# Transformer block on one core: x turned by VectorE and on-chip transfers instead of TensorE, all engine orders laid anew

## The chip, the cores and the metric

The kernel runs on one core of a Trainium2 chip. A core has five engines that run their own instruction streams and wait for each other by semaphores: TensorE (PE; its weight loads are shown as PEld), VectorE (DVE), ScalarE (ACT), GpSimd (POOL) and SyncE (SP), which here only issues transfers. The metric is the device time of one launch in microseconds (us), the median of several runs.

## The reference

For each of 32 batches of 256 tokens with 128 features, in float32:

```python
x = x + layernorm(attention(layernorm(x), Wqkv, Wo))
x = x + layernorm(tanh(layernorm(x) @ weight @ aux_weight1 @ aux_weight2 + bias))
```

Attention has 8 heads of 64. Wqkv (1536x128) gives q, k and v; a table of sines and cosines is added to q and k; scores = q k^T / 8 with a causal mask, softmax, times v; Wo (128x512) brings the 512 head values back to 128. The layernorms have no weights, epsilon is 1e-5.

## The kernel before, in words

A batch's 256 tokens are two tiles of 128 rows, so most tiles are 128 partitions by 2 x 128 columns. The 8 heads are worked in two units k = 0, 1 of two pairs j = 0, 1 of two heads each.

What happens to a batch b, with the function of each step:

- SP loads x twice, into `x_in` (for the norm) and later `x_res` (for the residual). DVE takes mean and variance (`stats_x`, `take_moments`), POOL makes 1/sqrt(var + eps) and writes the normalised `xn` (`norm_x`).
- PE turns `xn` with two 128x128 transposes into `misc_bank` (`turn_x`, by `turn_rows`, L941). ACT copies the result rounded to `xt_hi` (`keep_x_hi`, L307) and DVE writes the remainder `xt_lo` (`keep_x_lo`, L681). The two parts let q, k and v be computed in the fast format with three products each (`make_qk`, L896 to L898; `make_vals`, L867 to L869).
- `make_qk(b, k, j)` fills the one `qk_bank`; DVE adds the sine table and frees it (`keep_qk`, L643). `make_scores` (L881) writes two score banks; DVE masks and takes the row maximum (`row_max`, L633), ACT takes the exponentials and row sums (`exps`, L265), DVE inverts the sums.
- The probabilities are scaled by the inverse sums: of pair 0 by DVE (`scale_probs`, L659), of pair 1 by POOL (L423).
- PE turns each pair's probabilities in 12 transposes of 64-row blocks (`turn_probs`, L921), ACT copies them out (`keep_turned`, L283 and L285), PE multiplies with v (`make_heads`, L935). The heads of unit 0 are copied out by DVE (`keep_heads`, L669), those of unit 1 by ACT (L295). The turned probabilities and the heads share two PSUM banks, so each `turn_probs` of pair 0 waits for the copy of the heads before it.
- `make_attn` (L996) multiplies with Wo into `misc_bank`; ACT copies it (`keep_attn`, L331), DVE takes statistics and normalises (`norm_attn`), POOL adds the residual (`make_x1`, L482).
- The second half: DVE statistics, POOL normalises (`norm_y`), PE turns y (`turn_y`), ACT copies (`keep_y`), PE multiplies with the three weights fused into one (`make_ffn`), ACT takes tanh, DVE statistics, POOL normalises and adds (`norm_ffn`, `make_out`), SP stores.

Every engine has its order written out by hand: a `begin`, a `slot(b, k)` for each batch and unit, in which neighbouring steps belong to different batches (b+2 for the norm of x, b-3 for the last norm), and an `end`. `all_slots` runs the first four batches straight, the middle ones in a loop of two batches, and the last one by `end`. An engine executes its list in order: whatever waits holds up all that stands behind it. `misc_bank` is shared by x turned, v, y turned, the feed-forward product and the attention product.

Of the kernel before, what the change touches and what calls it, by code (L numbers as in the profile page):

```python
# [7 lines left out]
ALU = mybir.AluOpType  # L8
# [6 lines left out]
P = 128  # L15
# [7 lines left out]
class Batch:  # L23
# [39 lines left out]
def build_block(nc, x, w_qkv_t, w_o_t, w1_t, w2, w3, bias, out, H):  # L63
# [17 lines left out]
    with ExitStack() as ctx:  # L81
# [32 lines left out]
        half_power, eps = sb("half_power", [P, TT]), sb("eps", [P, TT])  # L114
# [7 lines left out]
        xt_hi, xt_lo = two("xt_hi", [P, T], F32R), two("xt_lo", [P, T], F32R)  # L122
        vals = two("vals", [P, TT, F])
# [27 lines left out]
        x_turned, x_hi_kept, x_lo_kept = sem("x_turned"), sem("x_hi_kept"), sem("x_lo_kept")  # L151
        attn_made, attn_kept, x1_made, out_made = sem("attn_made"), sem("attn_kept"), sem("x1_made"), sem("out_made")
# [41 lines left out]
        def _(sp):  # L194
# [7 lines left out]

            def slot(b, k):
                if k == 0 and b.plus(3).exists():

                    wait(sp, norms["x"]["normed"], b.times(1, 2))
                    load(b.plus(3), x_in, x_loaded)
                if k == 0 and b.plus(1).exists():

                    wait(sp, x1_made, b.times(1))  # L210
                    load(b.plus(1), x_res, res_loaded)
                if k == 1 and b.plus(-2).exists():
                    c = b.plus(-2)
                    sp.wait_ge(out_made, c.times(1, 1))
                    sp.dma_start(rows(out_dram, c), x2[c.parity][:, :, :]).then_inc(stored[c.parity], 16)

            load(first, x_in, x_loaded)
            sp.dma_start(ident[:, :], ident_dram).then_inc(ident_in, 16)
            sp.dma_start(pe[:, :], pe_dram).then_inc(pe_in, 16)
            sp.dma_start(mask[:, :], mask_dram).then_inc(mask_in, 16)  # L220
# [8 lines left out]
            sp.dma_start(wo[:, :, :], w_o_t.rearrange("(c f) e -> f c e", f=P)).then_inc(wo_in, 16)  # L229
            for b in range(-1, 4):  # L230
                for k in range(2):
                    slot(Batch(b // 2, b % 2, B), k)
# [4 lines left out]
            for b in range(B - 4, B + 2):  # L237
                for k in range(2):
                    slot(Batch(b // 2, b % 2, B), k)
# [5 lines left out]
        def _(act):  # L245
            for i in range(3):
                part = slice(i * F, (i + 1) * F)
                act.dma_start(w_raw[:, part], w_qkv_t[:, part]).then_inc(w_in[i], 16)
# [19 lines left out]

            def keep_vals(b, t):
# [18 lines left out]
            def keep_heads(b):  # L288

                if not b.exists():  # L290
                    return
                act.wait_ge(heads_made, units(b, 2))

                wait(act, attn_made, b.times(1, -1))
                nc.scalar.copy(heads_t[b.parity][:, 2:4, :], heads_bank[:, :].rearrange("p (j t) -> p j t", j=2)  # L295
                               ).then_inc(heads_kept[1], 1)

            def keep_x_hi(b):
                if not b.exists():
                    return  # L300
                act.wait_ge(x_turned, b.times(1, 1))

                wait(act, y_turned, b.times(1, -2))
# [3 lines left out]
                nc.scalar.copy(xt_hi[b.parity][:, :], misc_bank[:, 0:T]).then_inc(x_hi_kept, 1)  # L307
# [803 lines left out]
```

## Time and profile before

| | |
|---|---|
| median of 3 runs | 556.6 us (556.47 to 557.93) |
| profiled execution, device time | 557.18 us |
| its span, first to last instruction | 555.3 us |
| PE busy | 523.5 us, 94% of the span |
| DVE busy | 468.8 us, 84% |
| ACT busy | 410.9 us, 74% |
| POOL busy | 398.9 us, 72% |
| mean granted TensorE clock | 0.982 of full |

The profile is of one execution. Around the span lie 1.9 us in which no engine runs an instruction (557.18 - 555.3). Busy is the time in which at least one instruction of the engine runs; a busy PE includes the filling and emptying of its pipeline, so PE's busy share stays high even in short stalls, and the starts of its groups of matmuls tell more than its busy time.

### The profile page before, as it was taken

The page shows a single profiled execution, that of the slowest core. Times are in us where ns is not written, and L with a number is a line of the kernel's source. Part 1 is how long each engine was busy: PE and PEld are TensorE (multiplying, and loading weights), DVE is VectorE, ACT ScalarE, POOL GpSimd, SP SyncE. Part 2 cuts the span into 40 slices and gives each one's busy share as a digit, 9 for nine tenths or more (in the row PEclk, how much of TensorE's full clock was granted, in tenths as well). Part 3 has the DMA queues.
Part 4 walks back from the last instruction along what each step waited for, and adds up shares of the span by engine and source line. Part 5 has one row for each costly group of instructions (what it writes and reads, how often), then busy time and mean ns, then how long its engine had stood idle before and what let it go on. Part 6 is the DMA issues. An engine that isn't in the chain of part 4 may idle for free.

```text
span 555.3 us, 18471 instructions
## 1 busy us (share of the span) xinstructions
PE 523.5 (94%) x5363; PEld 427.2 (77%) x5363; DVE 468.8 (84%) x2063; ACT 410.9 (74%) x1507; POOL 398.9 (72%) x650
## 2 busy tenths in 40 slices
PE   8799999999999999999999999999999999999771
PEld 4588888788888878888887887888788888878650
DVE  4988898888889888888988888898888889888723
ACT  2777878778787877878787787877778787777730
POOL 3535777777777777777778777777877777785644
PEclk9999999999999999999999999999999999999966
DMA  5100011100001010000101010010000001100000
GB/s 161 30 2 21 11 31 30 30 19 28 20 18 28 28 28 19 28 26 12 28 28 28 19 28 21 17 28 28 28 19 28 26 12 28 28 19 12 21 11 19
DMA packets 27964, 14.57 MB, mean 26 GB/s; under 512 B 1699, under 2 KB 27430, under 8 KB 27942
## 3 DMA queue, kind: packets, MB, share of 16 engines
q1 hardware_dynamic: 27510, 13.51, 8.5%
q10 hardware_dynamic: 432, 0.79, 0.4%
q8 instruction: 11, 0.18, 0.1%
q14 instruction: 11, 0.09, 0.1%
HBM read 10.09 MB, written 4.19 MB: 26 GB/s over the span
## 4 chain that ended last, share of the span: by engine, by line
PE 82%; ACT 9%; issue 4%; DVE 3%; DMA 1%; POOL 1%; ACTq 0%; POOLq 0%; DVEq 0%
PE turned_and_heads L935 17%; PE scores L881 15%; PE misc_bank L996 11%; PE turned_and_heads L921 9%; PE qk_bank L896 6%; ACT probs L265 5%; PE qk_bank L898 4%; PE qk_bank L897 4%; PE misc_bank L867 4%; PE misc_bank L979 3%; PE misc_bank L869 3%; PE misc_bank L868 3%; ACT vals L275 2%; ACT pt L285 1%; PE misc_bank L977 1%
## 5 line engine op out<-in xcount | busy, mean ns | idle before, releaser
L265 ACT ACTIVATE probs<-scores,neg_max 128x256 f32<-128x256 f32 (+1 forms) x512 | 209.3, 428 | 32.0 <-DVE neg_max L633 31.9
L633 DVE CUSTOM_DVE_ANT_0 scores<-scores,mask 128x256 f32<-128x256 f32 (+1 forms) x512 | 166.2, 386 | 3.2 <-PE scores L881 0.9
L643 DVE TENSOR_TENSOR qk<-qk_bank,pe 128x512 f32<-128x512 f32 x128 | 87.4, 683 | 32.9 <-PE qk_bank L898 25.3
L881 PE MATMUL scores<-qk 64*128 64x256 f32 (+1 forms) x1024 | 107.2, 337 | 5.5 <-ACT probs L265 2.5
L423 POOL TENSOR_TENSOR probs<-probs,inv_sum 128x512 f32<-128x512 f32 x126 | 101.6, 827 | 12.8 <-DVE inv_sum L649 12.8
L265 ACT ACTIVATION_READ_ACCUMULATOR probs<-scores,neg_max 128x1 f32 x512 | 108.8, 213 | 0.0
L881 PEld LDWEIGHTS scores<-qk 64*128 64x128 f32 x1024 | 88.5, 188 | 16.0 <-issue 9.8
L935 PE MATMUL turned_and_heads<-pt,vals 128*64 128x256 f32 (+1 forms) x1024 | 99.3, 337 | 1.5 <-ACT pt L285 1.5
L935 PEld LDWEIGHTS turned_and_heads<-pt,vals 128*64 128x64 f32 x1024 | 64.8, 138 | 28.3 <-issue 2.8
L283 ACT COPY pt<-turned_and_heads 128x512 f32<-128x512 f32 x128 | 76.7, 599 | 11.1 <-PE turned_and_heads L921 11.0
L896 PE MATMUL qk_bank<-xt_hi,w_hi 128*128 128x256 f32 x256 | 81.2, 317 | 2.0 <-DVE qk L643 1.2
L921 PEld LDWEIGHTS turned_and_heads<-ident,probs 64*128 64x128 f32 x1536 | 58.5, 140 | 30.0 <-issue 22.1
L921 PE MATMUL turned_and_heads<-ident,probs 64*128 64x64 f32 x1536 | 75.9, 232 | 4.7 <-ACT pt L285 3.5
L659 DVE TENSOR_TENSOR probs<-probs,inv_sum 128x512 f32<-128x512 f32 (+1 forms) x128 | 77.2, 643 | 0.0
L633 DVE DVE_READ_ACCUMULATOR2_ANT neg_max<- 128x1 f32 x512 | 71.8, 140 | 0.0
L898 PE MATMUL qk_bank<-xt_hi,w_lo 128*128 128x256 f32 x256 | 71.4, 279 | 0.0
L897 PE MATMUL qk_bank<-xt_lo,w_hi 128*128 128x256 f32 x256 | 71.3, 279 | 0.0
L996 PE MATMUL misc_bank<-wo,heads_t 128*128 128x128 f32 x512 | 65.1, 280 | 0.6 <-ACT ffn_th L322 0.6
L996 PEld LDWEIGHTS misc_bank<-wo,heads_t 128*128 128x128 f32 x512 | 59.6, 191 | 5.6 <-issue 3.9
L896 PEld LDWEIGHTS qk_bank<-xt_hi,w_hi 128*128 128x128 f32 x256 | 48.0, 188 | 12.3 <-issue 7.7
L285 ACT COPY pt<-turned_and_heads 128x256 f32<-128x256 f32 x128 | 51.0, 398 | 0.0
L275 ACT COPY vals<-misc_bank 128x512 f32<-128x512 f32 x64 | 39.4, 616 | 15.2 <-PE misc_bank L869 15.2
(87 smaller groups left out, 863.2 us busy)
## 6 DMA issues: line engine op xcount, KB each, us to landing
x_in<-in_x SPq DMA_DIRECT2D x32, 128.0 KB, 2.2
x_res<-in_x SPq DMA_DIRECT2D x32, 128.0 KB, 2.1
out_x<-x SPq DMA_DIRECT2D x32, 128.0 KB, 1.8
w_raw<-in_w_qkv_t ACTq DMA_DIRECT2D x3, 256.0 KB, 3.7
pe<-pe_table SPq DMA_DIRECT2D x1, 256.0 KB, 5.6
wo<-in_w_o_t SPq DMA_DIRECT2D x1, 256.0 KB, 4.0
mask<-causal_mask SPq DMA_DIRECT2D x1, 128.0 KB, 5.5
w_sb<-in_w SPq DMA_DIRECT2D x2, 64.0 KB, 3.8
```

Source lines behind the costliest of these rows:

```text
L265: ins = nc.scalar.activation(probs[k][j][:, h, lo:hi], s_bank[j][:, h, lo:hi], ACT.Exp, bias=neg_max[k][j][:, i:i + 1], scale=-1.0, accum_ ...
L423: ins = nc.gpsimd.tensor_tensor(some, some, inv, ALU.mult)
L633: ins = nc.vector.tensor_tensor_reduce(some, some, mask[:, t * P:2 * P], -1.0, HIGHEST, ALU.add, ALU.min, neg_max[k][j][:, i:i + 1])
L643: nc.vector.tensor_tensor(qk[j][:, :], qk_bank[:, :], pe[:, :], ALU.add).then_inc(qk_kept, 1)
L659: ins = nc.vector.tensor_tensor(some, some, inv, ALU.mult)
L881: ins = mm(s_bank[j][:, h, at:at + k_hi], qk[j][r, q_lo:q_lo + P], qk[j][r, T:T + k_hi], start=(at == 0), stop=True, skip_group_check=True)
L896: mm(to, w_hi[:, f], hi[:, :], start=True, stop=False)
L897: mm(to, w_hi[:, f], lo[:, :], start=False, stop=False)
L898: ins = mm(to, w_lo[:, f], hi[:, :], start=False, stop=True)
L921: ins = nc.tensor.transpose(turned_banks[:, f, n * D:(n + 1) * D], some[r, h, lo:lo + P], ident[r, r])
L935: ins = mm(heads_bank[h * D:(h + 1) * D, to], vals[b.parity][:, s, f:f + D], rhs[j][:, h, :], start=(s == 0), stop=(s == 1))
L996: ins = mm(misc_bank[:, t * E:(t + 1) * E], heads_t[b.parity][:, p, t * P:(t + 1) * P], wo[:, p, :], start=(p == 0), stop=(p == PAIRS - 1))
```

## The change

What it does, part by part:

1. **x turned without PE.** For every batch but the first, DVE transposes `xn` in 32x32 blocks in place of each block (`turn_x_blocks`, one instruction of 128x256), and SP issues 16 transfers within SBUF, one for each block position (i, j), that move block (j, i) of `x_blocks` to (i, j) of `xt` (`move_x`). Each moves 32 partitions x 2 x 32 floats. `keep_x_hi` and `keep_x_lo` read `xt` in SBUF, not `misc_bank`. PE's `turn_x` remains for batch 0 alone, and steps that shared `misc_bank` with it lose that wait.
2. **Scaling of pair 0** goes from DVE (two instructions a unit) to ACT (four a unit, in place).
3. **The copy of unit 1's heads** goes from ACT to DVE.
4. **All orders** of `slot`, `begin` and `end` are written anew on all five engines. Loads and stores on SP are one batch later or share the slot with `move_x`.
5. **Start:** the exponential's table is loaded by a dummy instruction; the first two thirds of the weights are loaded by SP, identity, mask and Wo by ACT; the first `make_qk` waits for the parts of the weights one by one.
6. **End:** the last attention product is written to `qk_bank`, without waiting for `misc_bank`; 31 products of zeros (`warm_up`) are placed among PE's last steps, where there were none; at the start there are 17 for 15.

The core of the diff (the orders of `end` and of POOL are left out):

```diff
+            def move_x(b):
+                if not b.exists() or b.is_below(1):
+                    return
+                sp.wait_ge(x_blocked, b.times(1))
+                parts = [slice(n, n + 32) for n in range(0, P, 32)]
+                for i in parts:
+                    for j in parts:
+                        sp.dma_start(xt[b.parity][i, :, j], x_blocks[b.parity][j, :, i]).then_inc(x_moved[b.parity], 16)
...
             def slot(b, k):
+                if k == 0:
+                    load_x(b.plus(3))
+                    load_res(b)
+                else:
+                    move_x(b.plus(2))
+                    store(b.plus(-3))
...
+            def scale_probs(b, k):
...
+                act.wait_ge(inv_found, pairs(b, k, 1))
+                for t, (lo, hi) in enumerate(((0, T), (T, SC))):
+                    for h in range(2):
+                        some, i = probs[k][0][:, h, lo:hi], 2 * t + h
+                        ins = nc.scalar.mul(some, some, inv_sum[k][0][:, i:i + 1])
+                ins.then_inc(scaled[0], 1)
...
-                act.wait_ge(x_turned, b.times(1, 1))
-                wait(act, y_turned, b.times(1, -2))
+                    wait_moved(act, b)
...
+            def turn_x_blocks(b):
...
+                dve.wait_ge(norms["x"]["normed"], b.times(1, 1))
+                if not b.is_below(3):
+                    wait_moved(dve, b.plus(-2))
+                nc.vector.transpose(x_blocks[b.parity][:, :, :], xn[b.parity][:, :, :]).then_inc(x_blocked, 1)
```

The new order of a batch on ACT, in the names of the code (b is the slot's batch; slot k = 0, then k = 1): exps(b-1,1,0), keep_y(b-3), exps(b-1,1,1), keep_turned(b-1,0,0), tanh(b-3), scale_probs(b-1,1), keep_turned(b-1,0,1), keep_attn(b-2); exps(b,0,0), exps(b,0,1), keep_vals(b,0), keep_turned(b-1,1,0), keep_x_hi(b+1), scale_probs(b,0), keep_turned(b-1,1,1), keep_vals(b,1).
On POOL: norm_y(b-2), norm_x(b+2), scale_probs(b,0), norm_ffn(b-3); scale_probs(b,1), rstd_attn(b-1), make_out(b-3), make_x1(b-1).

PE in the middle of the kernel, before: from the transposes of x to the second score group of a unit. The names in brackets are the semaphores waited for.

```order
L941 MATMUL misc_bank<-ident,xn 128x128 [waits vals_kept,x_normed]
L941 MATMUL misc_bank<-ident,xn 128x128
L941 MATMUL misc_bank<-ident,yn 128x128 [waits vals_kept,y_normed]
L941 MATMUL misc_bank<-ident,yn 128x128
L921 MATMUL turned_and_heads<-ident,probs 128x64 [waits pt1_kept,scaled1,pt0_kept]
L921 MATMUL turned_and_heads<-ident,probs 128x64 x11
L881 MATMUL scores<-qk 128x256 [waits exps_done,qk_kept]
L881 MATMUL scores<-qk 128x256
L881 MATMUL scores<-qk 128x128 x2
L881 MATMUL scores<-qk 128x256 [waits exps_done,qk_kept]
```

And the same stretch of PE after:

```order
L977 MATMUL turned_and_heads<-ident,probs 128x64 [waits heads_kept0,pt1_kept,scaled0,pt0_kept]
L977 MATMUL turned_and_heads<-ident,probs 128x64 x11
L934 MATMUL scores<-qk 128x256 [waits exps_done,qk_kept]
L934 MATMUL scores<-qk 128x256
L934 MATMUL scores<-qk 128x128 x2
L934 MATMUL scores<-qk 128x256 [waits exps_done,qk_kept]
L934 MATMUL scores<-qk 128x256
L934 MATMUL scores<-qk 128x128 x2
L977 MATMUL turned_and_heads<-ident,probs 128x64 [waits pt1_kept,scaled1,pt0_kept]
L977 MATMUL turned_and_heads<-ident,probs 128x64 x11
L920 MATMUL misc_bank<-w_hi,xt_hi 128x512 [waits vals_kept]
```

The transposes of x are gone, and the scores of unit 1 now stand between the two groups of turned probabilities, ahead of the second half of v.

DVE in the middle, before: the last rows of a batch's unit 1.

```order
L633 ISA neg_max 128x1
L569 BN_STATS attn_stats<-attn 128x6 x2
L649 RECIPROCAL inv_sum<-row_sum 128x4
L582 BN_AGGR attn_moments<-attn_stats 128x2 x2
L659 TENSOR_TENSOR probs<-probs,inv_sum 128x2x256
L659 TENSOR_TENSOR probs<-probs,inv_sum 128x2x128
L643 TENSOR_TENSOR qk<-qk_bank,pe 128x512
```

After, the last rows of a batch's unit 1 on DVE:

```order
L636 BN_AGGR ffn_moments<-ffn_stats 128x2 x2
L711 COPY heads_t<-turned_and_heads 128x512
L731 STREAM_TRANSPOSE x_blocks<-xn 128x256
L697 TENSOR_TENSOR qk<-qk_bank,pe 128x512
L703 RECIPROCAL inv_sum<-row_sum 128x4 x2
```

The two scaling instructions are gone; the heads copy and the block transpose stand ahead of the `keep_qk` that the next scores wait for.

SP in the loop, after (one of its two batches):

```order
L214 DMA x_in<-in_x 128x2x128
L50 ISA
L214 ISA
L214 DMA x_res<-in_x 128x2x128
L240 DMA xt<-x_blocks 32x2x32 x16
L245 ISA
L246 ISA
L246 DMA out_x<-x 128x2x128
```

Before, the same queue held the two loads and the store alone; now 16 transfers stand between them.

## Rows read from the trace of the kernel before

**Rows 1.** The page's line of busy times of the engines

```profile
PE 523.5 (94%) x5363; PEld 427.2 (77%) x5363; DVE 468.8 (84%) x2063; ACT 410.9 (74%) x1507; POOL 398.9 (72%) x650
```

**Rows 2.** Windows, one batch in mid-run and the tail: span, busy, clock, DMA share, GB/s

```profile
254.70:270.90 16.20, 15.93 (x169) 13.13 (x167) 14.57 (x65) 12.76 (x49) 12.30 (x21) 1.00 0.09 24
...
520.00:535.00 15.00, 9.83 (x108) 7.70 (x105) 8.95 (x40) 8.42 (x32) 10.62 (x18) 0.78 0.03 9
```

**Rows 3.** Timeline of PE over one batch: start, us, engine, line, operation, count

```profile
254.71 0.38 PE L896 MATMUL qk_bank<-xt_hi,w_hi 128*128 128x256 f32 x1
...
257.64 0.38 PE L941 MATMUL misc_bank<-ident,xn 128*128 128x128 f32 x2
257.86 0.38 PE L941 MATMUL misc_bank<-ident,yn 128*128 128x128 f32 x2
258.17 0.59 PE L921 MATMUL turned_and_heads<-ident,probs 64*128 64x64 f32 x12
258.60 1.94 PE L881 MATMUL scores<-qk 64*128 64x256 f32 x16
...
265.30 0.59 PE L921 MATMUL turned_and_heads<-ident,probs 64*128 64x64 f32 x12
266.01 0.47 PE L867 MATMUL misc_bank<-w_hi,xt_hi 128*128 128x512 f32 x1
...
268.01 1.52 PE L881 MATMUL scores<-qk 64*128 64x256 f32 x16
...
270.91 0.39 PE L896 MATMUL qk_bank<-xt_hi,w_hi 128*128 128x256 f32 x1
```

**Rows 4.** Groups by line and form: busy us, mean ns of one, idle before

```profile
L659 DVE TENSOR_TENSOR probs<-probs,inv_sum 128x512 f32<-128x512 f32 x64 | 46.5, 727 | 0.0
L659 DVE TENSOR_TENSOR probs<-probs,inv_sum 128x256 f32<-128x256 f32 x64 | 35.7, 558 | 0.0
L669 DVE COPY heads_t<-turned_and_heads 128x512 f32<-128x512 f32 x32 | 22.1, 691 | 1.6 <-PE turned_and_heads L935 1.3
...
L681 DVE TENSOR_TENSOR xt_lo<-misc_bank,xt_hi 128x256 fp32r<-128x256 f32 x32 | 13.6, 424 | 9.5 <-ACT yt L314 6.0 <-ACT xt_hi L307 2.5
...
L265 ACT ACTIVATE probs<-scores,neg_max 128x256 f32<-128x256 f32 x256 | 119.8, 477 | 32.0 <-DVE neg_max L633 31.9
...
L410 POOL TENSOR_TENSOR ffn_n<-ffn_th,ffn_moments 128x256 f32<-128x256 f32 x31 | 26.7, 860 | 4.4
```

**Rows 5.** Timelines of ACT, then of POOL, in the same batch

```profile
257.47 0.38 ACT L285 COPY pt<-turned_and_heads 128x256 f32<-128x256 f32 x1
257.74 0.49 ACT L265 ACTIVATE probs<-scores,neg_max 128x256 f32<-128x256 f32 x1
...
265.40 0.37 ACT L331 COPY attn<-misc_bank 128x256 f32<-128x256 f32 x1 [0.71 <-PE misc_bank L996]
...
255.02 0.20 POOL L400 TENSOR_TENSOR y_var_eps<-y_moments,eps 128x2 f32<-128x2 f32 x1
...
256.85 0.61 POOL L412 TENSOR_TENSOR yn<-yn,y_rstd 128x256 f32<-128x256 f32 x1
...
269.20 0.73 POOL L482 TENSOR_TENSOR x<-attn_n,x_res 128x256 f32<-128x256 f32 x1 [0.96 <-DVE attn_n L617]
```

**Rows 6.** Transfers issued by SP at the start; loads from issue to landing

```profile
1.24 0.46 SPq L218 DMA_DIRECT2D ident<-identity  x1
...
3.17 0.94 SPq L225 DMA_DIRECT2D bias_raw<-in_bias  x3
...
x_in<-in_x SPq DMA_DIRECT2D x32, 128.0 KB, 2.2
```

**Rows 7.** Timeline of PE: batch 1's first group, `end`'s first, the last attention product

```profile
28.32 0.38 PE L896 MATMUL qk_bank<-xt_hi,w_hi 128*128 128x256 f32 x1
...
513.92 0.50 PE L867 MATMUL misc_bank<-w_hi,xt_hi 128*128 128x512 f32 x1
...
539.43 2.02 PE L996 MATMUL misc_bank<-wo,heads_t 128*128 128x128 f32 x16 [0.56 <-ACT ffn_th L322]
```

More of the change, by code:

```diff
@@ L38, in is_first, with is_below @@
         return isinstance(self.half, int) and 2 * self.half + self.parity == 0
+    def is_below(self, n):
+        return isinstance(self.half, int) and 2 * self.half + self.parity < n
     def exists(self):
@@ L201, in load, with load_x @@
                 sp.dma_start(dst[b.parity][:, :, :], rows(x_dram, b)).then_inc(loaded[b.parity], 16)
-            def slot(b, k):
[L204 to L215, printed above, removed]
+            def load_x(b):
+                if not b.exists() or b.is_below(2):
+                    return
+                wait(sp, norms["x"]["normed"], b.times(1, -1))
+                load(b, x_in, x_loaded)
@@ L217, in _, with store @@
+            def store(b):
+                if not b.exists():
+                    return
+                sp.wait_ge(out_made, b.times(1, 1))
+                sp.dma_start(rows(out_dram, b), x2[b.parity][:, :, :]).then_inc(stored[b.parity], 16)
+            def slot(b, k):
+                if k == 0:
[4 more added lines that the diff above has]
+                    store(b.plus(-3))
             load(first, x_in, x_loaded)
-            sp.dma_start(ident[:, :], ident_dram).then_inc(ident_in, 16)
+            for i in range(2):
+                part = slice(i * F, (i + 1) * F)
+                sp.dma_start(w_raw[:, part], w_qkv_t[:, part]).then_inc(w_in[i], 16)
@@ L228, in _ @@
             sp.dma_start(w3_sb[:, :], w3).then_inc(ffn_in, 16)
-            sp.dma_start(wo[:, :, :], w_o_t.rearrange("(c f) e -> f c e", f=P)).then_inc(wo_in, 16)
-            for b in range(-1, 4):
+            for b in range(-3, 4):
                 for k in range(2):
@@ L236, in _ @@
                         slot(Batch(half, parity, B), k)
-            for b in range(B - 4, B + 2):
+            for b in range(B - 4, B + 4):
                 for k in range(2):
@@ L725, in scale_last @@
             def scale_last():
+                dve.wait_ge(scaled[1], units(last, 1))
                 dve.wait_ge(inv_found, pairs(last, 1, 2))
@@ L892, in make_qk @@
                 for part in range(2):
+                    if b.is_first() and k == 0 and j == 0:
+                        pe_eng.wait_ge(w_hi_made, part + 1)
+                        pe_eng.wait_ge(w_lo_made, part + 1)
                     p = 2 * k + j
```

324 lines of the change are left out of this document (172 added, 152 removed).

## The prediction, made before the changed kernel ran

> **What bounds the kernel now.** I read the busy line first: PE 94%, the others 72 to 84% [rows 1]. Then one batch in mid-run: between two equal groups of PE lie 16.20 us (270.91 - 254.71), with PE busy for 15.93, DVE 14.57, ACT 12.76, POOL 12.30 at full clock [rows 2, 3]. The whole run confirms the pace: batch 1's first group starts at 28.32 and `end` at 513.92, 30 batches later, so 16.19 each [rows 7]. The span is a head of 28.3, 30 x 16.19 = 485.6 and a tail of 41.4.
>
> PE is the bound, but not all of its 16.20 is work. The two score groups of a batch have the same 16 instructions; one takes 1.52, the other 1.94, so 0.42 is a wait inside it. A group of 12 probability transposes takes 0.43 to the next group (258.17 to 258.60), but 0.71 where v's first product follows it and waits for the attention copy (265.30 to 266.01): 0.28. The transposes of x take 0.22 (257.64 to 257.86) [rows 3]. Floor of the new list of PE's work: 16.20 - 0.42 - 0.28 - 0.22 = 15.28, say 15.3. With the old order and x still on PE it would be 15.5.
>
> **The change, part by part, for one batch in mid-run.**
>
> *x off PE*: -0.22 of PE's work, counted above. On DVE one 128x256 transpose is added. The trace has none; the nearest row is the 128x256 `xt_lo` at 0.42, the upper end the 128x512 heads copy at 0.69, the lower 0.3 [rows 4]. I take 0.42.
>
> *Scaling of pair 0*: DVE loses two instructions a unit, 0.727 + 0.558, in two units 2.57 [rows 4]. It gains the transpose and one heads copy, 0.42 + 0.69. DVE's load becomes 14.57 - 2.57 + 1.11 = 13.1: no bound. ACT gains two instructions of 256 columns and two of 128 a unit. Lower bound: a copy of 256 columns lets the next start 0.27 later (257.47 to 257.74) [rows 5], and half the columns cannot take less than half, 2 x 0.27 + 2 x 0.135 = 0.8 a unit. Upper bound: as long as the 256-column exponential throughout, 4 x 0.477 = 1.9 [rows 4]. I take 1.0, near the copy, as there is no sum to read out. ACT's load: 12.76 - 0.6 (the heads copy that it gives up) + 2.0 = 14.2, with bounds of 13.8 and 16.0.
>
> *Contention*: DVE's 256-column scaling, both inputs in SBUF, takes 0.558, where `xt_lo`, as many columns with one input in PSUM, takes 0.424; POOL's subtraction that runs beside it has a mean of 0.86, against 0.61 of its like on y [rows 4, 5]. The Trainium skill (SBUF — State Buffer, "Who interferes with whom") says that a VectorE instruction with two SBUF inputs and a GpSimd one that reads SBUF lock each other out. By that rule POOL gets back some 0.25 at each such meeting. I leave it out of the sum; the new `xt_lo` has two SBUF inputs and takes part of it back.
>
> *The new orders*: I walk the batch with a = the end of an attention product on PE, counting durations and about 0.1 for each handover. Two loops go from one attention product to the next.
> POOL's loop: from the attention copy to the end of x1 the old trace needs 269.93 - 265.40 = 4.5 [rows 5]; a DVE heads copy now stands in it, so 4.7. Statistics of y and of the last norm, 1.2. `norm_y` is 2.44 (255.02 to 257.46) [rows 5]; `norm_x`, the same four instructions, now stands directly behind it, 2.44. Block transpose and `keep_qk`, 1.1; second half of the scores, probability transposes, attention product, 3.2 together. Sum 15.1.
> ACT's loop: attention copy 0.4, two sets of exponentials 3.2, v 0.6, turned pair 0.75 (it waits for PE to about a + 4.6), `xt_hi` 0.3, scaling 1.0, turned 0.75, v 0.6, exponentials 1.6, y 0.4, exponentials 1.6, turned 0.75, then the last transposes and the product 2.45; with the 0.7 of waiting for PE, 15.1. If ACT's scaling is 1.3 a unit, 15.4.
>
> Both fall just under PE's 15.3, with 0.2 to spare. Three loops so close cannot all hide each other's delays. The old kernel lies 0.7 above its floor while ACT has 3.4 us free; the new one has 2 fewer, but an order that starts each step early. I take half of that loss, 0.3: **15.6 us a batch**, with 15.3 and 16.0 as bounds.
>
> *The transfers*: 16 issues on SP. In the old trace three tiny ones take 0.94, 0.31 each; the identity's is 0.46 [rows 6]. At 0.4 each, 6.4; the loads land 2.2 after issue [rows 6], so about 8.6 from the block transpose to `xt`, bounds 7.2 and 9.6. By the walk `xt` is wanted 9.4 after the transpose: hidden, with 0.8 in hand, and nothing at 9.6 beyond 0.2. Also on SP, the next load of x and the residual stand behind the 16 and behind the store; both are wanted over 5 us after they can go. The store's wait holds them about as long as before. `misc_bank`'s lost waits give nothing beyond the removed 0.28.
>
> *The head*: batch 1's x now has to pass DVE, 16 issues and a landing before its first q and k. The block transpose of batch 1 stands in DVE's `begin` behind the fused weights, at about 14.6; + 8.7 = 23.3, then `xt_hi`, `xt_lo`: PE's first group of batch 1 at about 24, which in steady order lies 4 us into its batch, with less work before it. The next batch begins by my walk at 33 where it was 28.3: +4.8, of which 0.8 is work that `begin` takes over.
>
> *The tail*: walked from `end`: the scores of the last unit start 2.6 after its begin; the last attention product ends at about 20, where it ended 541.45 - 513.92 = 27.5 after [rows 7]. I allow 1 for what I missed: -6.5. The tail's clock was granted at 0.78 [rows 2]; the products of zeros stand in PE's idle time there. The old tail shows 0.78 with PE idle for a third of the stretch. If they hold full clock, the steps after the attention product shorten by 0.6. Tail: 41.4 - 7 = 34.3.
>
> **Sum.** Head 33.1, 30 x 15.6 = 468.0, tail 34.3: span 535.4. With the 1.9 around it 537.3; the profiled execution lay 0.6 above its median, so **536.7 us**, 3.6% faster. About 24 us, of which 17.7 is mid-run.
>
> **Rivals.**
>
> *A, the transfers become the bound (slower).* There is no row of a transfer within SBUF or of rows of 128 bytes. A block transpose can start only after `xt_hi` and the steps behind it: `xt_hi`, `xt_lo`, q and k, `keep_qk`, row maximum, heads copy, transpose: about 5.0. So the batch cannot be shorter than 5.0 + the time from transpose to landing. With 0.4 an issue this is 13.6. The kernel is slower than before when the batch is over 16.3 ((555.3 - 67.4)/30), that is when the 16 take over 11.3, or 0.57 an issue with 2.2 of landing. At 0.65 an issue: 12.6 + 5.0 = 17.6, and 67.4 + 528 + 1.3 = **597 us**. Against it: the issues in the rows cost 0.31 to 0.46, and the one of a whole 128-row table costs hardly more than those of a single row [rows 6]. Chance 0.10.
> The Trainium skill (DMA: Bandwidth & Descriptors, "Specifications") wants 512 bytes for full rate and speaks of read-modify-write below; its section "Why small descriptors are slow (HBM only)" exempts transfers within SBUF. These rows are of 128 bytes. By the first a landing takes more than the loads' 2.2, and each us beyond 3.0 lengthens the batch by A's rule up to one us, 30 us in all; by the second nothing is added. No row here shows either.
>
> *B, ACT becomes the bound.* Scaling on ACT at the upper bound makes ACT's load 16.0, and its loop 15.1 + 0.9 = 16.0 at least. Then 67.4 + 480 + 1.3 = **549 us**, still faster. For it: ACT now has 14 to 15 instructions' worth of work between each attention product and the next with hardly a gap. Against it: plain copies here cost 0.27 a step. Chance 0.15.
>
> *C, nothing is lost over the floor.* The batch is 15.3: 67.4 + 459 + 1.3 = **528 us**. For it: every consumer in the walk has 0.1 to 0.8 in hand. Against it: the old order also looks free of waits on paper and is not. Chance 0.20.
>
> *D, new stalls eat the gain.* The wait goes from the score banks to another place (the block transpose waits for `norm_x`, and `keep_qk`, scores, attention product wait behind it), and the batch stays at 16.1: 67.4 + 483 + 1.3 = **552 us**. Chance 0.05, with the transfer reaching 0.5 an issue among it.
>
> **How the numbers follow.** The forecast has 0.50, A 0.10, B 0.15, C 0.20, D 0.05. The range takes in C and B and leaves out A, most of D: 527 to 550 us. Of cases that end within 0.3% (1.7 us, about what a measurement of this kernel can tell from no change) there is only the upper edge of D and the lower of A: 0.02. Slower 0.09, faster 0.89.
>
> **What would show it.** In the new trace: equal groups of PE 15.6 apart in mid-run; ACT busy for about 14.2 of them, DVE for 13.1; the block transpose at about 0.4 and each ACT scaling at 0.3 to 0.4; 16 issues in 6 to 7 us and the last landing under 9.4 after the transpose; `xt_hi` waiting for PE or ACT's order, not for a transfer. Batch 2 and not batch 1 in full pace; the last attention product some 21 us after `end` begins. I am wrong if ACT waits for `xt`, if SP needs over 0.55 an issue, or if the scores or probability transposes wait over 0.5 in each batch.

## The result, and the profile after

The changed kernel takes **596.0 us** (median of 4 runs, 595.3 to 598.5); the kernel before took 557.3 in the same session. The ratio is 1.069 [1.066, 1.073]: 7% slower, where 3.6% faster was forecast. It is rival A's case, and close to its figure of 597 us.

The page after: busy line, granted clock, the two lines of the chain, and the line of the moves. They answer to [rows 1] and the landing in [rows 6].

```profile
PE 524.1 (88%) x5334; PEld 431.9 (73%) x5334; DVE 446.3 (75%) x1998; ACT 472.9 (80%) x1732; POOL 375.6 (63%) x650
...
PEclk9778899998999998989999999999999999999999
...
SPq 36%; PE 23%; DVE 12%; issue 10%; DMA 8%; ACT 6%; POOL 3%; DVEq 1%; POOLq 0%; ACTq 0%
SPq L240 35%; DMA xt<-x_blocks 7%; PE turned_and_heads L991 6%; DVE scores L687 4%; PE scores L934 4%; PE misc_bank L1054 3%; PE turned_and_heads L977 3%; ACT probs L320 2%; DVE x_blocks L731 2%; DVE neg_max L687 2%; PE qk_bank L952 1%; ACT xt_hi L352 1%; PE qk_bank L953 1%; PE qk_bank L954 1%; DVE heads_t L711 1%
...
xt<-x_blocks SPq DMA_DIRECT2D x496, 8.0 KB, 1.8
```

PE has fallen from 94% to 88%, and no engine has taken its place. What leads the chain is SP's queue: 35% of the span is line 240, the issuing of the moves, and 7% more their landing. Mid-run, SP's timeline (start, time, what):

```profile
279.82 10.21 SPq L240 DMA_DIRECT2D xt<-x_blocks  x16
290.32 0.41 SPq L246 DMA_DIRECT2D out_x<-x  x1
291.03 0.39 SPq L214 DMA_DIRECT2D x_in<-in_x  x1
...
297.02 1.25 SPq L240 DMA_DIRECT2D xt<-x_blocks  x2
```

The 16 issues take 10.21, **0.64 each**; the loads behind them, of 16 times the bytes, take 0.39. The other half of the loop is on VectorE and ScalarE; DVE's timeline, then ACT's, in the same batch:

```profile
279.35 0.45 DVE L731 STREAM_TRANSPOSE x_blocks<-xn 128x256 f32<-128x256 f32 x1 [0.19 <-POOL xn L466]
...
287.51 1.01 DVE L671 SCALAR_TENSOR_TENSOR attn_n<-attn,attn_moments,attn_rstd 128x128 f32<-128x128 f32 x2
...
292.04 0.73 DVE L721 TENSOR_TENSOR xt_lo<-xt,xt_hi 128x256 fp32r<-128x256 f32 x1 [1.30 <-ACT xt_hi L352]
294.00 0.69 DVE L697 TENSOR_TENSOR qk<-qk_bank,pe 128x512 f32<-128x512 f32 x1
...
295.99 0.66 DVE L711 COPY heads_t<-turned_and_heads 128x512 f32<-128x512 f32 x1
296.56 0.43 DVE L731 STREAM_TRANSPOSE x_blocks<-xn 128x256 f32<-128x256 f32 x1
```

```profile
291.41 0.40 ACT L352 CAST xt_hi<-xt 128x256 fp32r<-128x256 f32 x1 [1.78 <-PE misc_bank L922]
291.72 1.49 ACT L320 ACTIVATE probs<-probs,inv_sum 128x256 f32<-128x256 f32 x4
293.12 0.56 ACT L337 COPY pt<-turned_and_heads 128x512 f32<-128x512 f32 x1
```

Follow it round: block transpose 279.35, first issue 279.82, last issue done 290.03, `xt_hi` 291.41, `xt_lo` 292.04, `keep_qk` 294.00, heads copy 295.99, next block transpose 296.56. That is 17.21, of which 12.06 from transpose to `xt_hi` and 5.15 behind it. The label on `xt_hi` names PE, but PE had long been done: the time fits the last landing (289.4 + 1.8 = 291.2). The list of waits over the whole run has it right:

```profile
ACT xt_hi L352 <- DMA xt<-x_blocks: 48.8, 26, 5.8
...
PE qk_bank L952 <- DVE xt_lo L721: 37.3, 30, 3.7
```

Four batches between batch 3 and the end are longer still. Two of the stretches between the products of the feed-forward layer, one a batch (PEclk is the last column but two), show what happens there:

```profile
243.53:262.70 19.17, 16.95 (x168) 14.06 (x166) 14.22 (x63) 14.74 (x55) 14.90 (x25) 0.91 0.12 27
262.70:279.33 16.63, 15.56 (x167) 12.93 (x166) 13.57 (x62) 14.59 (x55) 9.44 (x17) 1.00 0.14 32
```

PE is busy for 16.95 where the same matmuls take 15.56: the granted clock was 0.91. The two batches together take 35.8, 1.9 more than two of the batches without a fall, which take 16.93 on average. Four such pairs cost some 6 us of the 594. What brings the falls on was not found: PE waits 1.1 to 1.7 us in most batches here, and 1.3 to 1.6 in after_short below, where no fall shows after the first batches.

### The profile page after: what moved, and what is told of

Same layout as the page of the kernel before. It is cut to its first block, busy times and chain, and to the rows that moved or that the text cites. A ratio compares the mean times of both kernels' runs of the same rounds, so it can differ in the third digit from the quotient of the medians.

```text
span 594.1 us, 18960 instructions
## 1 busy us (share of the span) xinstructions
PE 524.1 (88%) x5334; PEld 431.9 (73%) x5334; DVE 446.3 (75%) x1998; ACT 472.9 (80%) x1732; POOL 375.6 (63%) x650
## 4 chain that ended last, share of the span: by engine, by line
SPq 36%; PE 23%; DVE 12%; issue 10%; DMA 8%; ACT 6%; POOL 3%; DVEq 1%; POOLq 0%; ACTq 0%
SPq L240 35%; DMA xt<-x_blocks 7%; PE turned_and_heads L991 6%; DVE scores L687 4%; PE scores L934 4%; PE misc_bank L1054 3%; PE turned_and_heads L977 3%; ACT probs L320 2%; DVE x_blocks L731 2%; DVE neg_max L687 2%; PE qk_bank L952 1%; ACT xt_hi L352 1%; PE qk_bank L953 1%; PE qk_bank L954 1%; DVE heads_t L711 1%
## 5 line engine op out<-in xcount | busy, mean ns | idle before, releaser
L687 DVE CUSTOM_DVE_ANT_0 scores<-scores,mask 128x256 f32<-128x256 f32 (+1 forms) x512 | 166.3, 386 | 10.2 <-PE scores L934 6.4
L991 PE MATMUL turned_and_heads<-pt,vals 128*64 128x256 f32 (+1 forms) x1024 | 103.7, 347 | 13.9 <-ACT pt L339 13.4
L308 ACT ACTIVATION_READ_ACCUMULATOR probs<-scores,neg_max 128x1 f32 x512 | 114.0, 223 | 0.0
L934 PE MATMUL scores<-qk 64*128 64x256 f32 (+1 forms) x1024 | 103.2, 340 | 0.0
L991 PEld LDWEIGHTS turned_and_heads<-pt,vals 128*64 128x64 f32 x1024 | 69.6, 143 | 43.1 <-issue 12.1
L320 ACT ACTIVATE probs<-probs,inv_sum 128x256 f32<-128x256 f32 (+1 forms) x256 | 96.3, 466 | 0.0
L952 PEld LDWEIGHTS qk_bank<-xt_hi,w_hi 128*128 128x128 f32 x256 | 50.3, 196 | 59.1 <-issue 28.3
L953 PE MATMUL qk_bank<-xt_lo,w_hi 128*128 128x256 f32 x256 | 73.6, 288 | 0.0
L977 PEld LDWEIGHTS turned_and_heads<-ident,probs 64*128 64x128 f32 x1536 | 60.6, 140 | 12.9 <-issue 4.3
L352 ACT CAST xt_hi<-xt 128x256 fp32r<-128x256 f32 x31 | 12.5, 405 | 57.6 <-DMA xt<-x_blocks 48.8
L454 POOL TENSOR_TENSOR attn_var_eps<-attn_moments,eps 128x2 f32<-128x2 f32 x32 | 6.2, 195 | 77.9 <-DVE attn_moments L636 77.9
```

The costliest lines, as they stand in the source:

```text
L308: ins = nc.scalar.activation(probs[k][j][:, h, lo:hi], s_bank[j][:, h, lo:hi], ACT.Exp, bias=neg_max[k][j][:, i:i + 1], scale=-1.0, accum_ ...
L320: ins = nc.scalar.mul(some, some, inv_sum[k][0][:, i:i + 1])
L687: ins = nc.vector.tensor_tensor_reduce(some, some, mask[:, t * P:2 * P], -1.0, HIGHEST, ALU.add, ALU.min, neg_max[k][j][:, i:i + 1])
L934: ins = mm(s_bank[j][:, h, at:at + k_hi], qk[j][r, q_lo:q_lo + P], qk[j][r, T:T + k_hi], start=(at == 0), stop=True, skip_group_check=True)
L952: mm(to, w_hi[:, f], hi[:, :], start=True, stop=False)
L953: mm(to, w_hi[:, f], lo[:, :], start=False, stop=False)
```

## The experiments

In all of them "a batch" is the distance between two products of the feed-forward layer on PE, which stand once in each. The kernel before, on the same chip, took 558 to 559 us each time.

### What an issue costs

**m1_issue_costs**: transfers alone, nothing beside them.

> No part of the reference is computed; the output is a copy of x. SP issues transfers of 11 shapes in groups, each group waited for: a) 16 of 32x2x32 within SBUF to other partitions, b) the same to the same partitions, c) 32x64, d) 32x2x64, e) 128x2x32, f) 128x16, g) 16x64, h) 32x64 from DRAM, i) 32x2x128 from DRAM, j) 32x2x128 within SBUF, k) 32x256 as one row; ACT then issues 16 of shape a. DVE transposes one 128x256 and 16 single 32x2x32 blocks to other partitions; POOL copies 16 such blocks. Theory 1 (an issue costs by what its source and shape are, 0.64 us for the small on-chip ones whatever stands around them): a is 0.60 to 0.64 a piece, and c, h or k, with fewer dimensions or from DRAM, near 0.3 to 0.45. Rival (an issue is slow in the changed kernel because the engines and the other queue disturb it): a is 0.3 to 0.45 here too. Landing after the last issue 1.8 to 2.2 in all. A single block transpose on DVE 0.12 to 0.2, a copy on POOL 0.15 to 0.3.

SP's timeline, one row a group (start, time of the whole group):

```profile
2.93 10.37 SPq L42 DMA_DIRECT2D dst<-src  x16
...
14.50 10.17 SPq L45 DMA_DIRECT2D dst<-src  x16
...
38.43 2.69 SPq L54 DMA_DIRECT2D dst<-src  x4
...
48.64 5.00 SPq L60 DMA_DIRECT2D dst<-src  x8
54.81 3.59 SPq L63 DMA_DIRECT2D dst<-in_x  x8
...
66.69 2.41 SPq L72 DMA_DIRECT2D dst<-src  x4
```

L42 is the kernel's own move, 32x2x32 to other partitions: 0.65 each, as in the kernel, so neither contention nor the loop makes it dear. L45 (same partitions), L54 (128x2x32), L60 (16x64, a quarter of the rows) and L72 (32x256, whole rows of 1 KB) all cost 0.60 to 0.67, so the cheap shapes that theory 1 hoped for (32x64, 32x256) are as dear; ACT's queue asks as much for L42's move (16 in 10.35). L63, 32x64 from DRAM, costs 0.45. For these shapes the price is one per instruction, whether it moves 4 KB or 32. I read from this that a source in SBUF is what makes it 0.64, and tested that next.

**dram16** puts one store ahead and lets the 16 moves read from DRAM; **dram4** does so with four; **m2_issue_costs** measures such forms alone.

```diff
+ sp.dma_start(x_dram_blocks[b.parity][:, :, :], x_blocks[b.parity][:, :, :]).then_inc(x_stored[b.parity], 16)
+ wait(sp, x_stored[b.parity], (b.half + b.parity) * 16)
# dram16: the 16 moves as before, source x_dram_blocks
# dram4:
+ for i in parts:
+     sp.dma_start(xt[b.parity][i, :, :].rearrange("p t (j c) -> p t j c", c=32),
+                  x_dram_blocks[b.parity][:, :, i].rearrange("(j p) t c -> p t j c", p=32)).then_inc(x_moved[b.parity], 16)
```

> The changed kernel, with one thing changed: the 16 moves of blocks read a copy of the blocks in DRAM, which one more transfer has written before them (issued by SP ahead of the 16, which wait until it has landed). Number, shapes and destinations of the 16 stay. Theory 1 (an issue costs 0.64 us when its source is SBUF and 0.44 when it is DRAM, and SP's issues are on the loop that sets the pace): from the block transpose to the last landing 0.6 for the issue of the store, 2.0 for its landing, 16 x 0.44 = 7.0 and 1.8 for the last landing, 11.4 against 12.05; with the same 5.0 behind it a batch is 16.4 and the time 570 to 582 us, less than the changed kernel's 596 in spite of a seventeenth transfer and a wait for it. Theory 2 (the price is that of 16 small rows' descriptors, wherever they come from, or of 16 transfers in one queue): issues stay at 0.64, the path becomes 14.6 + 5.0 = 19.6, over 660 us. Theory 3 (the loop does not go through SP's issues at all): the time stays within 2 us of 596.

Measured: **672.6 us**, ratio 1.207 [1.202, 1.211]. My theory 1 fell, theory 2's figure came: SP's timeline has the store at 0.34, and the 16 from DRAM at 10.16, 0.64 each, no less than from SBUF:

```profile
275.92 0.34 SPq L239 DMA_DIRECT2D x_dram_blocks<-x_blocks  x1
277.64 10.16 SPq L244 DMA_DIRECT2D xt<-x_dram_blocks  x16
```

The batch is 19.5 on average, where theory 2 had 19.6. But that agreement is in part luck: of 25 batches in mid-run 18 take 19.7 to 20.4 us at a granted clock of 0.83 to 0.92, seven 17.7 to 18.2 at full clock, and the mean clock of the run is 0.92 against 0.97. So not all of the 77 us over the changed kernel are issues and the store's landing.

> A kernel of transfers alone, on SP, to see what sets the 0.64 us of an issue; its output is a copy of x. Groups: from a DRAM scratch 32x2x32 x16 (a), from the input 32x2x32 x16 (b), from the scratch 32x64 x8 (c), from the input 32x64 x8 (d), from the scratch 32x2x128 x4 (e) and 32x2x4x32, 256 rows of 128 bytes, x4 (f), SBUF to scratch 128x256, each waited for (g), scratch to SBUF 128x256 x4 (h), SBUF to scratch 32x2x32 x8 (i), within SBUF 128x256 x4 (j), within SBUF 32x2x32, each waited for (k), scratch 16x128 x8 (l), input 128x2x128, each waited for (m). Theory R (rows under 256 bytes make an issue dear whatever the source, and so does a source in SBUF): a, b, f, i at 0.6 or more, c, d, e, h, l, m at 0.35 to 0.45, j and k at 0.6. Theory S (a DRAM scratch is dearer than an input): a, c, e, f, h at 0.6, b, d, m at 0.45. Theory Q (issues back to back are dear, those that stand alone cheap): g, k, m at 0.35 to 0.45, the rest at 0.6, with d against it already (0.45 in a row of 8).

```profile
2.90 0.34 SPq L40 DMA_DIRECT2D scratch<-src  x1
4.63 10.24 SPq L43 DMA_DIRECT2D dst<-scratch  x16
16.38 7.39 SPq L46 DMA_DIRECT2D dst<-in_x  x16
25.09 3.57 SPq L49 DMA_DIRECT2D dst<-scratch  x8
...
37.82 2.54 SPq L58 DMA_DIRECT2D dst<-scratch  x4
```

Issued in a row, 4 to 32 KB each, the transfers have two prices, 0.43 to 0.46 and 0.60 to 0.67. The high one: everything within SBUF from 4 to 32 KB, and 32x2x32 blocks out of (L43) or into the scratch. The low one: 32x64 out of the scratch (L49), and 32x2x32 out of the input (L46), whose two tiles lie 64 KB apart and not 512 bytes. Each of the three theories has a group against it: R has b, S has c, and Q has k, which stands alone between waits and still takes 0.61. And size does not make an issue dear: standing alone, 128x256 out of the scratch (h, L65) and within SBUF (j, L71) take less than the small moves (ns, lowest, median, highest):

```profile
L65 SPq DMA_DIRECT2D dst<-scratch x4: 319/320/320, 49.0 to 54.8; - x4
L71 SPq DMA_DIRECT2D dst<-src x4: 465/490/552, 63.0 to 69.1; - x4
L74 SPq DMA_DIRECT2D dst<-src x4: 585/608/653, 71.1 to 76.5; - x4
```

What picks the price stays open. What it does not depend on is shown: L58 moves four times the blocks of L43 in one instruction (256 rows of 128 bytes) for the same 0.64.

> The changed kernel with the same blocks brought to the same places, by fewer transfers: one writes all turned blocks to DRAM, four read them back, each the four blocks of one group of 32 partitions (32x2x4x32, as many rows of 128 bytes in all as the 16 had). Theory 1 (the loss is SP's issue time of 16 transfers, on the loop): from the transpose to the last landing 0.34 + 1.8 for the store, 4 x 0.64 = 2.6 and 2.0, 6.7 against 12.05, so the loop of the transfers is 11.7 a batch and out of the way: as the kernel of 4 moves within SBUF, 543 to 549 us. Theory 2 (256 rows of 128 bytes are what costs, in however many instructions): 590 us or more.

Measured: **546.8 us**, ratio 0.978 [0.974, 0.981]. It computes all that the changed kernel does, brings the same rows of 128 bytes to the same places with an additional trip through DRAM, and is 49 us faster. dram16 differs from it only in that 16 reads do what 4 do here, and takes 126 us more. It is the number of instructions that costs, not the rows. These two runs settle the main cause.

**n12** and **n4** stay within SBUF and cut the number: 12 of 32x2x32 and 32x2x64, or 4 of 32x2x128. They leave the blocks in their own partitions.

```diff
- for j in parts:
-     sp.dma_start(xt[b.parity][i, :, j], x_blocks[b.parity][j, :, i]).then_inc(x_moved[b.parity], 16)
+ sp.dma_start(xt[b.parity][i, :, :], x_blocks[b.parity][i, :, :]).then_inc(x_moved[b.parity], 16)   # n4
```

> As the changed kernel, but x_blocks is brought to xt by 12 transfers (two of 32x2x32 and one of 32x2x64 for each 32 partitions) with all bytes moved and no block put in its place, so x is turned wrongly. Theory 1 (the loop block transpose, 16 issues, landing, xt_hi and on to the next block transpose is the bound: 5.0 + 16 x 0.64 + 1.8 = 17.0 a batch): with 12 it is 5.0 + 7.7 + 1.8 = 14.5, below PE's floor, and the batch falls from 17.3 to about 15.7, the run from 596 to 543 (535 to 552). Theory 2 (the new orders and ACT's scaling are the bound, the wait for the transfers only lies in it): the batch stays at 16.8 or more, the run at 580 or more.

> As the changed kernel, but with 4 transfers a batch (32x2x128 each, all bytes moved, no block put in its place). Theory 1: below the bound at 12 already, so the same as with 12 transfers within 4 us. Theory 2: 580 or more. A third (each issue costs in proportion, by SP's queue before loads and stores, with no threshold): from 16 to 12 a third of what 16 to 4 gives.

Measured: 548.7 (ratio 0.983 [0.980, 0.986]) and **546.3** (0.978 [0.975, 0.980]). Twelve are nearly as good as four: four instructions fewer, 2.6 us of issue, take 47 us off, and eight more 2.4. That is a threshold, as rival A has it (batch = 5.0 + transpose to landing, once this passes the other loops), and not a cost per transfer. n4 runs at 15.94 a batch, all alike.

### The rest of the forecast: scaling, and the loop of POOL

**x_on_pe** keeps the new orders and ScalarE's scaling and turns x on TensorE, two batches ahead. **scale_on_dve** is the same with pair 0 scaled by VectorE again. It is not quite the new orders alone: the copy of unit 1's heads stays on VectorE, and x is turned at another place than before.

> The new orders, ACT's scaling, start and end of the changed kernel, but x turned by PE again, two batches ahead between the feed-forward product and the turned probabilities; no block transpose, no transfers within SBUF. Computes all of the reference. Theory 1: the batch is PE's list of 15.3 + 0.22, with the small waits 15.7 to 15.9: 540 to 550, faster than before (557). Theory 2: ACT, whose scaling takes 1.4 a unit, or the orders bound it: 16.5 or more, 570 or more.

> The kernel with the new orders and x turned by TensorE (552.1 us), with pair 0 scaled by VectorE as in the kernel before (two instructions a unit, 0.73 + 0.56), not by ScalarE. It leaves the new orders alone as the only change to the kernel before (559). Theory 1: VectorE's load rises from 13.3 to 15.9 a batch and becomes the bound with what it waits: 16.3 to 16.9, 556 to 575 us; the ACT scaling is then worth 4 to 20 us. Rival (ACT's 2.9 a batch of scaling lies on ACT's loop and costs as much as it takes from VectorE): 545 to 552, the scaling by ScalarE was worth nothing.

Measured: **552.1** (0.989 [0.986, 0.992]), 16.1 a batch; and **598.6** (1.072 [1.068, 1.076]), 17.6 a batch. The first lies 2 us above theory 1's range and far below theory 2's 570; the second is far over the 575 that I allowed. Groups by form in scale_on_dve: VectorE's scaling, then POOL's of pair 1 beside it, and POOL's in x_on_pe:

```profile
L673 DVE TENSOR_TENSOR probs<-probs,inv_sum 128x256 f32<-128x256 f32 x64 | 56.7, 886 | 0.0
L673 DVE TENSOR_TENSOR probs<-probs,inv_sum 128x512 f32<-128x512 f32 x64 | 55.7, 870 | 0.1
...
L441 POOL TENSOR_TENSOR probs<-probs,inv_sum 128x256 f32<-128x256 f32 x63 | 51.4, 816 | 0.0
```

```profile
L457 POOL TENSOR_TENSOR probs<-probs,inv_sum 128x256 f32<-128x256 f32 x63 | 38.7, 614 | 0.0
```

A unit of VectorE's scaling costs 1.76 here, where it cost 1.28 before [rows 4], and POOL's 256 columns 0.82 instead of 0.61 on average. In this order unit 1's two scalings run side by side, which they did not before, and unit 0's runs beside POOL's output addition (1.13 where x_on_pe has 0.74). So in this kernel moving pair 0 to ScalarE is worth 46 us, but not for one reason. The stretching of VectorE's scaling is 0.94 of the 1.48 that a batch grows by. The load of 15.9 came as theory 1 had it, and does not fill the 17.6:

```profile
252.96:270.55 17.59, 15.79 (x169) 13.17 (x168) 15.88 (x68) 12.40 (x46) 12.64 (x21) 1.00 0.08 22
```

There is also a wait that x_on_pe does not have. `xt_lo` stands directly behind the scaling on VectorE, and the tanh on ScalarE waits for it, as x turned by PE shares `misc_bank`:

```profile
ACT ffn_th L337 <- DVE xt_lo L692: 19.6, 27, 1.7
```

That wait belongs to x on PE. What the scaling on VectorE would cost in the changed kernel itself was not run.

**out_first** swaps two lines of POOL in x_on_pe; **n4_swap** two of VectorE in n4.

```diff
# out_first, POOL                      # n4_swap, VectorE
- rstd_attn(b.plus(-1))                - turn_x_blocks(b.plus(2))
  make_out(b.plus(-3))                   keep_qk(b.plus(1), 0, 1)
+ rstd_attn(b.plus(-1))                + turn_x_blocks(b.plus(2))
```

> The kernel with the new orders and x turned by TensorE (552.1 us), with one swap on POOL: make_out(b-3) stands ahead of rstd_attn(b-1), not behind it. Theory C (make_out, a POOL addition with both inputs in SBUF, runs beside VectorE's two attn_n instructions, which take 0.52 each there against 0.30, and attn_n is on the loop that sets the pace): attn_n falls to 0.6 for both, the loop by 0.4, 30 x 0.4 = 12: 538 to 543 us. Rival (attn_n is off the loop, or the delay of rstd_attn behind make_out, 0.6, takes it back): within 2 us of 552, or slower.

> The kernel with 4 moves of 32x2x128 a batch, with one swap: on VectorE keep_qk(b+1, 0, 1) stands ahead of turn_x_blocks(b+2), not behind it. Theory L (with the moves short enough, what sets the 15.94 of a batch is the loop attention copy, moments, x1, norm_y, norm_x on POOL, block transpose, keep_qk, second half of the scores, attention product): the block transpose's wait for POOL (0.90 a batch) leaves the loop, POOL and the rest follow within the batch, which falls to 15.4 to 15.7, 530 to 540 us against 546.3. Theory P (PE's own work, the granted clock and waits elsewhere hold it): within 1.5 us of 546.3.

Measured: **542.7** (0.973 [0.970, 0.977]) and 540.8 (0.970 [0.967, 0.974]). VectorE's `attn_n` in x_on_pe, then in out_first:

```profile
L648 DVE SCALAR_TENSOR_TENSOR attn_n<-attn,attn_moments,attn_rstd 128x128 f32<-128x128 f32 x62 | 30.0, 522 | 5.5 <-POOL attn_rstd L437 4.0
```

```profile
L648 DVE SCALAR_TENSOR_TENSOR attn_n<-attn,attn_moments,attn_rstd 128x128 f32<-128x128 f32 x62 | 19.1, 349 | 5.8 <-POOL attn_rstd L437 4.1
```

With POOL's addition out of its way the same instruction takes 0.35 and not 0.52, the two 0.35 less, and 9.4 us are gained (30 x 0.35 = 10.5). By the Trainium skill (SBUF — State Buffer, "Who interferes with whom") a VectorE instruction with two SBUF inputs and a GpSimd one that reads SBUF lock each other out of a shared pair of ports; this pair of rows agrees. n4_swap falls short of its 530 to 540: the batch goes from 15.94 to 15.74 only. The wait in question, in n4 and in n4_swap (total, times, longest):

```profile
DVE x_blocks L730 <- POOL xn L465: 24.9, 27, 1.0
```

```profile
DVE x_blocks L730 <- POOL xn L465: 9.2, 26, 0.4
```

The wait shrank by 0.58 in each of these batches, and the batch by 0.20; what took the rest was not traced. Theory L had the direction, not the size.

**short_loop_a** and **short_loop_b** shorten that loop throughout, with x on TensorE; **dram4_short** is a's order with dram4's transfers and n4_swap's swap; **after_short** is a's order with the 16 moves.

```diff
 POOL, k == 0:                        POOL, k == 1:
+ norm_x(b.plus(2), rstd=False)       + make_out(b.plus(-3))
  norm_y(b.plus(-2))                    rstd_attn(b.plus(-1))
- norm_x(b.plus(2))                   - make_out(b.plus(-3))
                                      + rstd_x(b.plus(3))        # b: the rstd stays with norm_x
 VectorE: take_moments("attn") ahead of keep_qk(b, 1, 0), take_moments("y") ahead of stats_ffn
```

> A version meant to beat both: the new orders, x turned by TensorE, pair 0 scaled by ScalarE, make_out ahead of rstd_attn on POOL (542.7 us as it stands), and further on the loop of POOL: norm_x(b+2) ahead of norm_y, its rstd made in the batch before between rstd_attn and make_x1, the moments of the attention and of y on VectorE taken directly behind their statistics. If POOL's loop still holds the batch (its waits for y_moments, 1.4 a batch, and attn_moments, 1.0), 0.3 to 0.6 a batch is gained and TensorE's own work (15.3) sets the pace: 530 to 537 us. Rival (TensorE, 95% busy, and its other waits hold it already): 540 to 545.

> As short_loop_a, with the rstd of x made directly ahead of norm_x(b+2) and not in the batch before. If the 0.9 of an rstd between rstd_attn and make_x1 delays x1 and costs a's gain, this one is faster than a by 1 to 10 us; if x1 waits for attn_n there anyway, a is the faster one by 0 to 5.

Measured: **532.2** (0.952 [0.949, 0.955]) and 541.9 (0.970 [0.966, 0.974]). With a's other edits in place, nearly the whole of its gain over out_first lies in making x's rstd a batch early: with it directly ahead of `norm_x`, b is 9.7 us slower, more than either guess had. The early rstd without the other edits was not run. In a, the chain is "PE 92%" and its batch 15.34.

> The change with one store and four loads in place of its 16 moves (546.8), and with the shorter loop of POOL and VectorE that gave 532.2 with x turned by TensorE: make_out ahead of rstd_attn, rstd_x a batch early, norm_x ahead of norm_y, moments directly behind their statistics, and the block transpose of x behind keep_qk(b+1, 0, 1). Theory 1 (the transfers cost nothing once they are few; what kept the kernel of four moves at 15.94 a batch was that loop): TensorE's floor without the turns of x, 15.1 to 15.3 a batch, is reached, 526 to 532 us. Rival (the turning on VectorE and the transfers cost more than TensorE's 0.2 to 0.3 a batch that they save, in the head above all, where batch 1 waits for them): 533 to 540.

> The changed kernel with its 16 moves within SBUF as they are, and the same shorter loop of POOL and VectorE (here the block transpose stays ahead of keep_qk). Theory 1 (the loop block transpose, 16 issues, landing, xt_hi, xt_lo, q and k, keep_qk, block transpose holds the batch, and POOL's loop is not in it): 585 to 597 us, no more than 10 us of gain. Rival (the two loops share a part, or POOL's loop was the bound in some of the batches): 560 to 584.

Measured: dram4_short **529.8** (0.947 [0.944, 0.950]), the fastest kernel of the study and one that computes all of the reference: 5.3% faster than before. Every batch takes 15.20 or 15.30. after_short: 589.3 (1.055 [1.050, 1.059]): the edits that, with the swap, took 17 us off dram4 took 6.6 off the changed kernel, with batches of 16.68 and 16.96 in turn. With the 16 moves in place POOL's loop is hardly worth mending. The busy line of dram4_short, and of after_short the wait that is still there:

```profile
PE 504.1 (95%) x5333; PEld 426.2 (81%) x5334; DVE 433.4 (82%) x1998; ACT 469.2 (89%) x1732; POOL 377.5 (71%) x652
```

```profile
ACT xt_hi L352 <- DMA xt<-x_blocks: 56.5, 31, 5.8
```

## Why the prediction was wrong, step by step

- **The transfers: the step that failed.** "16 issues on SP ... At 0.4 each, 6.4; ... about 8.6 from the block transpose to `xt`, bounds 7.2 and 9.6." Measured: 0.64 an issue, 10.2, and 12.06 from transpose to `xt_hi`, 2.5 over the upper bound. The landing was right (1.8 against 2.2). The bound itself was the fault. It rests on 0.46 as the dearest issue, which is not the dearest in the trace of before; Wo's stands among SP's transfers at the start:

```profile
5.50 0.54 SPq L229 DMA_DIRECT2D wo<-in_w_o_t  x1
```

  And every issue there is one between DRAM and SBUF, of another kind than the moves. Rival A named the deciding point, 0.57 an issue, and gave 597 us at 0.65. It deserved far more than 0.10, with that point a quarter above the 0.46 and 6% above a row that could be read. That its figure came within 1 us is partly luck: it has 7.4 too much mid-run (17.6 a batch for 17.35) and 6.2 too little at the head. The sentences on rows of 128 bytes came out harmless: the moves landed after 1.8, and dram4 brings as many such rows. The Trainium skill's exemption of transfers within SBUF (DMA: Bandwidth & Descriptors, "Why small descriptors are slow (HBM only)") agrees with that 1.8. It is no test of it: blocks with such rows out of DRAM landed after 1.8 to 2.0 in m2_issue_costs, so no run here shows the penalty that they are exempt from.
- **The sum.** The rows of PE for it: batch 1's first group, the first group of its own slot, the first of `end`, the last attention product [rows 7].

```profile
27.73 0.58 PE L952 MATMUL qk_bank<-xt_hi,w_hi 128*128 128x256 f32 x1 [3.73 <-DVE xt_lo L721]
...
39.26 0.28 PE L952 MATMUL qk_bank<-xt_hi,w_hi 128*128 128x256 f32 x1
...
559.85 0.59 PE L977 MATMUL turned_and_heads<-ident,probs 64*128 64x64 f32 x12
...
578.98 2.02 PE L1038 MATMUL qk_bank<-wo,heads_t 128*128 128x128 f32 x16
```

  From 39.3 to 559.85 lie 30 batches. The parts are 39.3 + 30 x 17.35 + 34.2 = 594.1, against 33.1 + 30 x 15.6 + 34.3 = 535.4. Of the 58.7 too many, 52.6 are mid-run, 6.2 the head, nothing the tail. Of the 52.6, 10.2 would be there with cheap transfers too (30 x (15.94 - 15.6), by n4); the other 42.4 came with the 16 moves, some 6 of them by the clock. The forecast's "about 24 us" of gain does not follow from its own sum: 556.6 - 536.7 is 19.9.
- **The head, +6.2.** PE's first group of batch 1 was foreseen at 24 and starts at 27.7, for the moves are issued from 15.3 to 25.6: 3.7 of the 6.2. Behind it PE's products take 0.41 each until 35.9 and 0.28 from there: the granted clock was 0.50 from 28 to 35.9, the lower of its two levels (1.2 GHz), after PE had waited 3.7 for `xt_lo`; dram4 has full clock from 28 to 36. What that costs of the other 2.5 was not taken apart.
- **The tail, right.** 34.2 against 34.3, the last attention product ending 21.2 after `end` begins, "some 21". The granted clock from `end` on was 0.98, where it was 0.76 before, as the forecast hoped of the products of zeros; no run takes them out.
- **PE's floor, right.** 15.3 foreseen; dram4_short runs at 15.25, short_loop_a, x on PE, at 15.34. But the turning of x, which the change takes off PE, then brings 0.09 a batch and not 0.22: dram4_short is only 2.4 us faster than a. dram4 is 5.3 faster than x_on_pe, but neither stands at PE's floor.
- **15.6 a batch without the transfers' cost: too low.** n4 and dram4 give 15.94, 546 us where 536.7 was forecast. POOL's loop, walked at 15.1, is the one: in n4's timelines it is 16.03 from one attention copy to the next (269.61 to 285.64). Its terms: from the copy to x1 5.1 for 4.7, as POOL's addition of the output runs right beside VectorE's two `attn_n` (1.01, where before has 0.61); the statistics of y and of the last norm 1.5 for 1.2; the two norms 4.95 for 4.88; block transpose and `keep_qk` 1.15 for 1.1; from there to the next copy 3.4 for 3.2. Rival D had the place (the block transpose waits for `norm_x`), at a price between the forecast's and its own: 15.94 lies between 15.6 and 16.1.
- **ScalarE.** A unit of scaling takes 1.40 (291.72 to 293.12), not 1.0, within the bounds of 0.8 and 1.9. ACT's load came to 14.6 against 14.2. Rival B, with 1.9 a unit, did not happen: dram4_short has the same scaling and a batch of 15.25.
- **Small prices, right.** Block transpose 0.44 (0.42 taken). VectorE is busy for 13.4 to 14.5 a batch (13.1), in part by contention.
- **Contention.** I left it out of the sum as a gain of POOL's. POOL had it: its subtraction for the last norm fell from 0.86 to 0.61. But VectorE paid elsewhere: 0.17 for each `attn_n`, beside `make_out`, worth 9 us in x_on_pe, and 0.11 for `xt_lo`, which now reads twice from SBUF (0.53 on average for 0.42) and stands on the loop of the transfers. In scale_on_dve the stretching of the scaling is 0.94 a batch, at most 28 of the 46 us.

## What to carry to other kernels

Price an operation that the trace does not show from both sides with room beyond the nearest rows, and when a rival needs only 40% more than your guess to turn the sign, and a quarter more than your bound, give it that weight. Transfers on a loop are to be counted by instruction: one store and four loads of many small rows beat 16 direct moves by 49 us. When one loop is removed look for the next by its waits, and try the order before the arithmetic: two lines swapped were worth 9 us, one small operation made a batch early, on top of other edits, 10.

## What the runs showed of the hardware

- An issue on SP's queue cost 0.60 to 0.67 us within SBUF, from 4 to 32 KB, in rows of 64 bytes to 1 KB (m1_issue_costs); on ACT's queue 0.65, and alone 0.61, both for 32x2x32. Within SBUF 128x256 took 0.49. Out of DRAM, in a row, it cost 0.43 to 0.46 or 0.64, by layout; 128x256, alone, 0.32 out of the scratch and 0.33 into it (m2_issue_costs).
- A single instruction can carry a four-dimensional pattern of 256 rows of 128 bytes for the same 0.64; it landed after 2.3 us (dram4, m2_issue_costs).
- VectorE's transpose of a 32x64 piece into other partitions took 0.25 (16 in 3.94, m1_issue_costs), and that of all of 128x256, each 32x32 block staying in its place, 0.44.
- Two instructions that each read two SBUF operands, one on VectorE and one on POOL, stretched each other: the scaling of 256 columns took 0.89 for 0.56 on VectorE and 0.82 for 0.61 on POOL (scale_on_dve against before and x_on_pe). `attn_n` took 0.52 for 0.35, while POOL's addition beside it took 0.74 and 0.73 (x_on_pe, out_first): there VectorE alone paid.
